# Graph network on one core: the sums of gathered rows stand three behind each group's read until they are used up, in place of two or three

## The reference, cut to what matters

```
def _gcn_conv(x, src, dst, W, b, n_nodes):
    h = x @ W
    loops = jnp.arange(n_nodes, dtype=src.dtype)
    s = jnp.concatenate([src, loops])
    d = jnp.concatenate([dst, loops])
    deg = jax.ops.segment_sum(jnp.ones_like(d, dtype=h.dtype), d, num_segments=n_nodes)
    dis = jnp.where(deg > 0, jax.lax.rsqrt(deg), 0.0)
    norm = dis[s] * dis[d]
    msg = h[s] * norm[:, None]
    out = jax.ops.segment_sum(msg, d, num_segments=n_nodes)
    return out + b
...
h = relu(_batch_norm(_gcn_conv(x, ..., W1, b1), g1, be1))
h = relu(_batch_norm(_gcn_conv(h, ..., W2, b2), g2, be2))
h = relu(_gcn_conv(h, ..., W3, b3))
h = _gcn_conv(h, ..., W3, b3)
```

## Time and profile before

| | us |
|---|---|
| median of 3 runs | 3914.21 (3911.45 to 3914.72) |
| the profiled execution | 3912.45 |
| its span | 3910.7 |
| TensorE busy | 3568.2 (91%) |
| VectorE busy | 2412.0 (62%) |
| GpSimd busy | 2355.3 (60%) |
| ScalarE busy | 1880.3 (48%) |

### The profile page before, as it was taken

One profiled execution on the slowest core, in us unless ns is written; L12 is line 12 of the kernel. 1 busy time (PEld: TensorE's weight loads), 2 busy tenths in 40 slices (PEclk: granted clock), 3 DMA queues, 4 the chain that ended last, 5 costly groups with the idle time before them and its releaser, 6 DMA issues. The chain is left out here.

```text
span 3910.7 us, 61608 instructions
## 1 busy us (share of the span) xinstructions
PE 3568.2 (91%) x21338; PEld 2113.7 (54%) x21338; DVE 2412.0 (62%) x3535; ACT 1880.3 (48%) x5147; POOL 2355.3 (60%) x2509
## 2 busy tenths in 40 slices
PE   5799999999999999999995889999999999989998
PEld 4566666666666666666663544444544454444444
DVE  8798888888889888888884764222422242224222
ACT  4787888888878788787882563000200020002000
POOL 2677777777777777777772003655365546544654
PEclk8798888888889888888886999999999999999999
DMA  6443333333333343333335017876887688768885
GB/s 204 128 107 106 103 107 106 106 106 104 106 105 106 103 107 106 106 107 102 107 106 92 36 30 230 249 239 187 255 251 244 184 257 253 240 192 254 254 248 172
DMA packets 497047, 606.58 MB, mean 155 GB/s; under 512 B 60201, under 2 KB 427140, under 8 KB 496478
## 3 DMA queue, kind: packets, MB, share of 16 engines
q1 hardware_dynamic: 358950, 341.00, 28.9%
q0 software_dynamic: 79968, 166.57, 17.4%
q10 hardware_dynamic: 57848, 95.46, 6.9%
HBM read 488.30 MB, written 116.12 MB: 155 GB/s over the span
## 5 line engine op out<-in xcount | busy, mean ns | idle before, releaser
L917 POOL DMA_INDIRECT fts<-ft_tab,src_all x1568 | 1479.5, 944 | 477.7 <-issue 477.4
L2290 PE MATMUL cv_acc<-cv_cnt,cv_parts 128*128 128x512 bf16 (+1 forms) x6468 | 1312.6, 367 | 0.0
L2290 PEld LDWEIGHTS cv_acc<-cv_cnt,cv_parts 128*128 128x128 bf16 x6468 | 616.6, 99 | 692.0
L2063 POOL DMA_INDIRECT cv_slots<-hs_tab,slot_idx x600 | 567.5, 946 | 473.0 <-issue 176.6
L954 DVE TENSOR_TENSOR ohk<-iota_ps,key_cols 128x784 bf16<-128x784 f32 x784 | 725.5, 967 | 6.1
L2124 DVE TENSOR_TENSOR cv_y<-cv_acc,dis_row 128x512 f32<-128x512 f32 (+1 forms) x52 | 34.4, 661 | 950.2 <-PE cv_acc L2290 924.4
L1047 ACT ACTIVATE dist_l<-lo_iota,low 128x128 bf16<-128x128 f16 x1960 | 593.7, 387 | 18.6 <-ACT low L1042 0.8
L1206 PE MATMUL agg_ps<-terms,oh 128*64 128x141 f32 x2744 | 530.5, 365 | 28.8 <-DVE terms L991 27.9
L1206 PEld LDWEIGHTS agg_ps<-terms,oh 128*64 128x64 f32 x2744 | 459.8, 181 | 84.1 <-DVE terms L991 71.3
L1099 ACT CAST strip<-adj_ps 128x392 bf16<-128x392 f32 x784 | 371.9, 474 | 275.2 <-PE adj_ps L1150 246.5
L1150 PE MATMUL adj_ps<-ohk,ohl 128*128 128x196 bf16 x3136 | 430.1, 262 | 0.0
(11 more groups left out here) (287 smaller groups left out, 3271.4 us busy)
## 6 DMA issues: line engine op xcount, KB each, us to landing
cv_cnt<-adj SPq DMA_DIRECT2D x88, 2048.0 KB, 9.3
cv_cnt<-adj SPq DMA_DIRECT2D x44, 2176.0 KB, 9.3
adj<-strip ACTq DMA_DIRECT2D x196, 392.0 KB
fts<-ft_tab,src_all POOLq DMA_INDIRECT x1568
win<-ft_tab SPq DMA_DIRECT2D x196, 65.0 KB
hs_tab<-cv_hs ACTq DMA_DIRECT2D x24, 448.0 KB, 3.8
cv_slots<-hs_tab,slot_idx POOLq DMA_INDIRECT x600
agg_tab<-res SPq DMA_DIRECT2D x196, 35.2 KB
```

What stands on the lines that cost most here:

```text
L917: nc.gpsimd.indirect_dma_start(fts[u][:, k, :], None, ft_tab[:, :], bass.IndirectOffsetOnAxis(src_all[:, n, k:k + 1], 0)).then_inc(gathere ...
L2063: nc.gpsimd.indirect_dma_start(slots[n % RING][:, e, :], None, hs_tab[:, :], bass.IndirectOffsetOnAxis(slot_idx[:, k, at:at + 1], 0)).then ...
L2290: last = nc.tensor.matmul(a[:, 0:width], parts[:, r, b, :], cnt[q][:, 0:width // SUB, (b - b0) * SUB:(b - b0 + 1) * SUB], start=(b == 0 an ...
```

## The change

A constant `PER_GROUP` = 3 replaces the formula. Behind group i stand blocks 3i to 3i+2 as long as there are any: three behind each of groups 0 to 8, block 27 alone behind group 9, none behind group 10. The number of sums, what each adds and every semaphore count stay. Since a line is added at the head of the file, lines of the kernel after are one higher.

```diff
 RING = 3
+PER_GROUP = 3
 DG = T0 * P // GRP
...
                         last = finish_group(i)
                         if l == L - 1 and i:
                             add_rows(i - 1)
-                        for b in range(NBK * min(i, DG) // DG, NBK * min(i + 1, DG) // DG):
+                        for b in range(min(NBK, PER_GROUP * i), min(NBK, PER_GROUP * (i + 1))):
                             add_slots(b)
                     if l < L - 1:
```

## The result

The changed kernel takes 3873.39 us (median of 4 runs, 3870.18 to 3873.91) against 3912.83 for the one before on the same chip: a ratio of 0.9898, 95% interval 0.9881 to 0.9915. Forecast were 3874.7 us within 3869 to 3885. In a later measurement the changed kernel took 3873.30 us against 3913.24, a ratio of 0.9895 (0.9878 to 0.9911).

What follows compares the result with a forecast made beforehand. TensorE was taken to bound the convolutions, waiting for VectorE's last sum each layer and then running at half clock. Wait 31.75 plus clock 7.8 gave 39.5 us off 3914.21: 3874.7 us, range 3869 to 3885.

Steps and rivals of the forecast that it cites:

- The wait: Layer ends: TensorE no longer waits for VectorE's last sum, so span 12's 147 narrow matmuls start earlier, 31.75 us in all.
- The clock: Span 12, the narrow matmuls ending each layer, runs at 2.4 GHz instead of partly half clock: 8.4 us each, 7.8 saved.
- GpSimd and the order: GpSimd's gathers, 1.252 us an issue, keep pace with three sums a group; the third sum costs nothing.
- Transfers: Groups 3 to 9 carry more gathers, 252 GB/s needed; the loads of counts still land in time, at no cost.
- the last chunk: Span 12's last load of counts lands about 2 us before use: nought, or 3.3 us a layer if slow.
- The rival of the transfers: Groups 3 to 9: transfers become the bound and TensorE waits for counts; 3939 us at 235 GB/s, chance 0.04.
- Behind span 12: Batch norm, next layer's loads and last output follow at the same distance; 3 us allowed either way.
- the 3 us allowed: Allowance, either way and in all, for the clock falling sooner or later at the start of a layer.
- "clock halves as before" rival: Layer ends: the wait goes, but span 12 still takes 10.3 us on average; 3882.5 us, chance 0.12.

Runs made afterwards that it cites:

- e1: Kernel before, sums behind groups 0 to 10 set to 3,3,3,3,3,3,3,3,1,0,3: early gathers, last three sums behind group 10; 3912.32 us, 0.9999 of before.
- e3: Kernel before with its wait kept, plus 130 unread matmuls of 128 columns on TensorE in that wait in layers 1 to 3; 3910.07 us, 0.9987 of before.
- e2: Kernel before, sums behind groups 0 to 10 set to 3,3,3,3,3,3,3,3,2,1,1: one left behind group 10; 3893.0 us, 0.9944 of before.
- e5: Changed kernel with PER_GROUP = 4: four sums behind each of groups 0 to 6, none later; 3969.0 us, 1.0147 of before.
- e4: Kernel before, sums behind groups 0 to 10 set to 2,3,2,3,2,3,2,3,2,6,0: none behind group 10, six behind group 9; 3908.95 us, 0.9987 of before.
- e6: Changed kernel plus unread matmuls before the first product of layers 1 to 3 (24, 60, 60); 3875.7 us, 0.9902 of before, beside 3873.30 for the changed kernel.

## Why the prediction was right

- *The wait, 31.75 us.* Span 12 starts at 2722.49 (forecast 2722.51), 3100.43, 3477.43 and 3857.33, in layers 1 to 3 some 0.95 us behind the start of the four transposes. TensorE's idle time fell by 30.8 us. e1 puts the sums back and has all of it back.
- *The clock, 7.8 us.* Span 12 takes 8.38, 8.38, 8.38 and 8.37 us (forecast 8.4), TensorE's busy time fell by 8.3, and e3 gets the same 8.37 with the wait left in. That the gap brings the clock down is shown from both sides: 0.35 us keeps it at 1.00, 3.7 us (e2) does not.
- *GpSimd and the order.* 1.252 us an issue without a stop, the last one 45 us ahead of group 10's end. Block 2's sum ended 1.6 us ahead of group 1's read; forecast were 2.0, with the end of its issues put 0.3 us too late (23 steps of 1.252 and 0.94 from 2784.64 give 2814.4, not 2814.7). The margin was small, but e5 shows that lateness below one group costs nothing.
- *Transfers.* 254 GB/s without a wait, counts landing in 9.1 to 9.3 us (medians), the last chunk 2 us early. The rival of the transfers failed at its first condition: groups 3 to 9 of the second layer take 31.73 us each, as before.
- *Behind span 12.* Of the 3 us allowed 0.4 were needed. By layers, from first product to first product, the gain is 9.5, 10.5, 9.3 and 9.8 us; by the sum, 9.6, 10.5, 9.7 and 9.7. What is missing in layer 3 lies at its start, 46.4 us from first product to group 1 where before it took 45.9. The second product of layer 2 took 2.82 us, at half clock for most of it, where before it had 1.80; it cost nothing, since that start took 47.3 us as before.
- *The number.* The gain is 39.4 us by the medians, forecast 39.5. That the time itself lies 1.3 us below the forecast is the median of before, which came out at 3912.83 with one more run, and not the change; agreement this close is partly luck, since the runs of one kernel spread over 4 us.

The "clock halves as before" rival would have given 3882.5. What it rested on, that span 12 had always started at half clock, was true of the kernel before only because of the wait. Behind a gap of 1.54 us, at the first product of layer 4, the changed kernel still has a clock of 1.00; gaps between that and 3.7 us were not tried.

## What to carry to other kernels

When the last of a series of small jobs stands behind the last big one, the whole pipeline can wait for it, however little the series weighs; take it from the slack of earlier rounds, and check that its inputs can be there by then (e4) and that the engine's lateness stays within its buffers (e5). A wait of TensorE is to be priced with the matmuls behind it, which may run at half clock: here that was a fifth of the gain. The same clock brought next to nothing where another engine sets the pace (e6), and matmuls added for its sake can themselves come in the way.

## What the runs showed of the hardware

- A gap of 3.69 us was enough to have the granted clock at 0.50 at the end of the gap in the first layer of e2, and span 12 then took 10.0 to 10.7 us in place of 8.4: as costly in clock as a gap of 8 us.
- In the second layer of e2 a gap as long left the clock at 1.00 up to its end, and it fell to 0.63 and 0.50 in the two microseconds behind it.
- The sum of a block, where VectorE stood waiting for its rows, began 1.5 to 5.7 us behind the end of the block's last issue in the second layer of e5: 4.9 for block 0, 5.7 for block 2, 1.6 for block 9, 5.6 for block 18 and 1.7 for block 27. What makes the difference stays open; the issues themselves came every 1.25 us throughout.
